# A two-layer graph kernel on one core: six tiles instead of ten between the adjacency scan and the first gather

## What is computed

```python
h = relu(layernorm(x))
# layer 0: attention by cosine of two projections, over the neighbours
raw = cosnorm(h @ Wk.T) @ cosnorm(h @ Wq.T).T
att = softmax(where(adj > 0, raw, NEG), axis=1)
prop = att @ h                       # h itself where a row has no neighbour
x = x + 0.5 * prop + 0.5 * h
# layer 1: attention by two vectors, over the same neighbours
h = relu(layernorm(x))
g = h @ W.T + b_W
e = leaky((g @ a1)[:, None] + (g @ a2)[None, :] + b_a, 0.2)
x = x + softmax(where(adj > 0, e, NEG), axis=1) @ g
```

## Time and profile before

| | |
|---|---|
| median of 3 runs | 1671.44 us (1669.94 to 1672.61) |
| the profiled execution: time | 1664.98 us |
| its span, first to last instruction | 1663.2 us |
| GpSimd (POOL) busy | 1120.6 us, 67% |
| TensorE busy (matmul) | 1140.0 us, 69% |
| VectorE busy | 1041.8 us, 63% |
| ScalarE busy | 891.0 us, 54% |
| adjacency loads on SyncE's queue | 256 of 1024 KB |
| indirect gathers issued by GpSimd | 1120 (576 + 544) |

### The profile page before, as it was taken

How to read it: one execution, slowest core, us unless ns; L and a number is a source line. 1 busy time by engine, 2 the same in 40 slices (tenths; PEclk the granted TensorE clock), 3 DMA queues, 4 the chain that set the end, 5 groups by cost and what they waited for, 6 DMA issues and landing times.

```text
span 1663.2 us, 22697 instructions
## 1 busy us (share of the span) xinstructions
PE 1140.0 (69%) x6317; PEld 898.4 (54%) x6317; DVE 1041.8 (63%) x4012; ACT 891.0 (54%) x2786; POOL 1120.6 (67%) x1170
## 2 busy tenths in 40 slices
PE   5877677777676677676556647666666767666765
PEld 3544344444444454454546537666666766666655
DVE  5976688888788887888763314444444444444444
ACT  3543455556556556556768735555555555555433
POOL 1224777777777767766777157777777777777775
PEclk9998788988989988889766657787878787878878
DMA  9999999999999999999222022222222222222222
GB/s 353 420 372 365 405 408 405 406 407 406 405 402 388 399 399 396 397 394 375 64 55 59 22 47 60 58 60 60 60 60 60 60 60 61 59 60 60 61 60 49
DMA packets 108396, 361.69 MB, mean 217 GB/s; under 512 B 24421, under 2 KB 57576, under 8 KB 75496
## 3 DMA queue, kind: packets, MB, share of 16 engines
q1 hardware_dynamic: 55272, 277.05, 41.4%
q0 software_dynamic: 35840, 74.62, 17.5%
q10 hardware_dynamic: 17152, 8.52, 1.9%
HBM read 347.38 MB, written 12.72 MB: 217 GB/s over the span
## 4 chain that ended last, share of the span: by engine, by line
POOL 35%; issue 12%; PE 2%; ACT 1%; DMA 0%; DVE 0%; POOLq 0%; ACTq 0%; DVEq 0%
POOL arena L559 18%; POOL arena L554 13%; POOL arena L968 4%; PE ps L1043 1%; PE ps L517 1%; ACT prod L1134 0%; DMA arena<-tab,idx_all 0%; PE ps L377 0%; ACT diag L1145 0%; PE ps L599 0%; DMA tab<-tw 0%; ACT arena L506 0%; ACT arena L508 0%; ACT arena L504 0%; ACT h L355 0%
## 5 line engine op out<-in xcount | busy, mean ns | idle before, releaser
L968 POOL DMA_INDIRECT arena<-tab,idx_all x576 | 564.0, 979 | 207.1 <-issue 167.7
L1012 PE MATMUL ps<-arena,fold 128*128 128x512 fp8e4 x1024 | 302.0, 427 | 194.4 <-DMA arena<-in_adj_dram 193.8
L559 POOL DMA_INDIRECT arena<-tab,idx_all x320 | 303.3, 948 | 97.5 <-issue 97.5
L554 POOL DMA_INDIRECT arena<-tab,idx_all x224 | 214.4, 957 | 111.7 <-issue 68.0
L1012 PEld LDWEIGHTS ps<-arena,fold 128*128 128x128 bf16 x1024 | 89.3, 102 | 360.2 <-DMA arena<-in_adj_dram 267.7
L1134 ACT ACTIVATE prod<-prod,arena 128x128 f32<-128x128 f32 x576 | 221.9, 388 | 34.3 <-DVE prod L1349 34.3
L686 DVE SCALAR_TENSOR_TENSOR arena<-ps,s_all,arena 128x512 f32<-128x512 f32 (+1 forms) x112 | 66.9, 633 | 252.0 <-PE ps L575 252.0
L575 PE MATMUL ps<-ident,arena 128*128 128x128 f32 x704 | 133.3, 358 | 77.6 <-DMA arena<-tab,idx_all 77.5
L517 PE MATMUL ps<-arena 128*128 128x26 f32 x704 | 103.9, 297 | 105.4 <-ACT keys L526 93.4
L629 ACT ACTIVATE arena<-arena,negm 128x517 f32<-128x517 f32 (+1 forms) x64 | 56.8, 887 | 216.4 <-DVE negm L696 216.4
L575 PEld LDWEIGHTS ps<-ident,arena 128*128 128x128 f32 x704 | 118.5, 258 | 82.7 <-DMA arena<-tab,idx_all 82.7
(11 more groups left out here) (200 smaller groups left out, 2205.2 us busy)
## 6 DMA issues: line engine op xcount, KB each, us to landing
arena<-in_adj_dram SPq DMA_DIRECT2D x256, 1024.0 KB
arena<-tab,idx_all POOLq DMA_INDIRECT x1120, 2.6
tab<-arena ACTq DMA_DIRECT2D x16, 260.0 KB, 14.5
tab<-tw ACTq DMA_DIRECT2D x32, 130.0 KB, 10.3
res<-in_x_dram SPq DMA_DIRECT2D x8, 512.0 KB, 6.6
out_dram<-arena SPq DMA_DIRECT2D x64, 64.0 KB, 1.6
prod<-in_L_gnn_Wq_dram SPq DMA_DIRECT2D x1, 64.0 KB
prod<-in_L_gnn_Wk_dram SPq DMA_DIRECT2D x1, 64.0 KB
```

The lines of the kernel that those rows point to most:

```text
L554: pool.indirect_dma_start(out=GS[h % 2][:, c, :], out_offset=None, in_=tab1, in_offset=bass.IndirectOffsetOnAxis(ap=idx_all[:, at, slot:sl ...
L559: pool.indirect_dma_start(out=GO[q][:, s, :], out_offset=None, in_=tab1, in_offset=bass.IndirectOffsetOnAxis(ap=idx_all[:, t, s:s + 1], ax ...
L968: pool.indirect_dma_start(out=G[q][:, s, :], out_offset=None, in_=tab0, in_offset=bass.IndirectOffsetOnAxis(ap=idx_all[:, t, s:s + 1], axi ...
L1012: last = nc.tensor.matmul(keys_ps[t % 2], fold[:, PIECE_BITS * f + b, :], ring8[m % RING][:, b * WORDS:(b + 1) * WORDS], start=False, stop ...
```

## The change

- `LEAD` is 3 and `AHEAD` 6: TensorE folds tile t + 7 in turn t, VectorE extracts t + 6.
- `early` has eight blocks, spread over the front (`1, 3, 4, 6, 8, 10, 12, 14`). Eight tiles are folded in the front, and only six of them extracted, decoded and compacted there; the other two wait in the two PSUM buffers. So the loop folds nothing in turns -1 and 0.
- The mask of a tile and its owner rows are made one tile later than before (`owner_mask(t + 2)`, `owners(t + 1)`); ScalarE copies the owner rows after its second-stage work; the count of the places (`offsets` on TensorE) stands before the second half of the fold.
- Own and spill slots of a gather have semaphores of their own, and GpSimd waits for the two halves of the index list apart, so the own half is gathered, multiplied and weighed without the other. `weighted` starts with the spill slots.
- Second layer: masks 0 to 3 are made on VectorE (new `masks1_vector`) in turns 64 and 65, their owner rows on TensorE in the same turns, copied at turn 66 and selected at 67. Masks 4 to 8 and their owner rows are made at the start of the second layer. `AT1` is 9, and each later selection comes one tile later on VectorE.
- The wait for the edge rows moves from the first `extract` to the end of the front.

```diff
-    AT1 = 10
+    AT1 = 9
-    LEAD = 5
+    LEAD = 3
     AHEAD = 2 * LEAD
-        edge_row = keys[0:1, :, 0:ROW]
+        edge_row = R[0][0:1, 0:2 * ROW].rearrange("p (a c) -> p a c", a=2)
...
+        def masks1_vector(dve, link, t):
+            first, n = span(t)
+            r, m = R1[t][:, 0:n * P], mask[t][:, 0:n * P]
+            nc.vector.tensor_scalar(r, iota1[:, 0:n * P], float(P * first), owner[:, t, OFF:OFF + 1], ALU.add,
+                                    ALU.is_ge).then_inc(s_R1, 1)
+            dve.wait_ge(s_R1, 3 * t + 1)
+            nc.vector.scalar_tensor_tensor(out=r, in0=iota1[:, 0:n * P], scalar=end4[:, t:t + 1], in1=r,
+                                           op0=ALU.is_lt, op1=ALU.mult).then_inc(s_R1, 1)
+            dve.wait_ge(s_R1, 3 * t + 2)
+            nc.vector.tensor_scalar(m, r, -1.0, -OUT, ALU.add, ALU.mult).then_inc(s_R1, 1)
...
+            for t in range(QT, AT1 - 1):
+                owners1_tensor(pe, t)
             edge_scores(0)
...
+            for t in range(QT, AT1):
+                masks1_scalar(act, t)
+                if t == 2 * QT - 1:
+                    copy_owners1_scalar(act, 1)
...
-        early = [1, 2, 4, 5, 6, 8, 9, 10, 12, 13]
-        assert len(early) == AHEAD and early[-1] < NB - 1
+        early = [1, 3, 4, 6, 8, 10, 12, 14]
+        assert len(early) == AHEAD + 2 and early[-1] < NB - 1
...
-                    pool.wait_ge(s_idx, 2 * t + 2)
                     if t >= GR:
                         pool.wait_ge(s_pv, t - GR + 1)
                     for s in range(SLOTS):
+                        if s in (0, K):
+                            pool.wait_ge(s_idx, 2 * t + 1 + s // K)
...
-                for t in range(-2, LAST):
-                    if t + 2 < T:
-                        owners(t + 2)
+                for t in range(-1, LAST):
+                    if t + 1 < T:
+                        owners(t + 1)
                     scan = t + AHEAD + 1
-                    if AHEAD <= scan < T:
+                    if AHEAD + 2 <= scan < T:
                         folds(scan, 0, PIECES // 2)
...
-                    if 60 <= t < 60 + AT1:
-                        owners1_tensor(pe, t - 60)
...
+                    if t in (T, T + 1):
+                        owners1_tensor(pe, 2 * (t - T))
+                        owners1_tensor(pe, 2 * (t - T) + 1)
...
-                    if 59 <= t < 59 + AT1:
-                        masks1_scalar(act, t - 59)
+                    if t == T + 2:
+                        copy_owners1_scalar(act, 0)
...
-                    if 2 <= t + 3 < T:
-                        owner_mask(t + 3)
+                    if 2 <= t + 2 < T:
+                        owner_mask(t + 2)
...
-                    if t in (65, 69):
-                        select1_vector(dve, link, (t - 65) // QT)
+                    if t in (T, T + 1):
+                        masks1_vector(dve, link, 2 * (t - T))
+                        masks1_vector(dve, link, 2 * (t - T) + 1)
+                    if t == T + 3:
+                        select1_vector(dve, link, 0)
```

More of the change, by code:

```diff
@@ L403, in adjacency_layers @@
         s_R, s_E, s_Eev, s_idx = sem("owner_mask"), sem("owner_rows"), sem("owner_rows_copied"), sem("idx_written")
-        s_g = [sem(f"l0_gathered_{q}") for q in range(GR)]
+        s_g = [[sem(f"{tag}_gathered_{q}") for q in range(GR)] for tag in ("own", "spill")]
         s_prod, s_red, s_ex = sem("l0_products"), sem("l0_scores"), sem("l0_weights")
@@ L1080, in _ @@
                         second.tensor_pr(pe, (t - 10) // 2)
-                    if AHEAD <= scan < T:
+                    if AHEAD + 2 <= scan < T:
                         folds(scan, PIECES // 2, PIECES)
-                    pair = (t + AHEAD - 3) // 2
-                    if t % 2 and LEAD <= pair < PAIRS:
-                        offsets(off_ps, pair, 1)
                 either(pe, rows_tensor, lists_tensor)
```

62 lines of the change are left out of this document (32 added, 30 removed).

## The result

The changed kernel took 1657.47 us (median of five runs, 1656.66 to 1662.78), the kernel before 1671.44 on the same chip: a ratio of 0.9929, 95% interval 0.9911 to 0.9946. On a second chip it was 0.9935 (0.9909 to 0.9961). By the ratio that is 12 us, by the medians 14 us, where 27 were forecast: inside the range of 1629 to 1664, but half the gain is missing.

A forecast was written before the change was run, and what follows sets the result against it. GpSimd's gathers were taken as the backbone, with the adjacency scan setting the pace beside it; -23 (gathers' end), -4 (drain) and 0 (second layer) made -27 us, from 1671.4 to 1644, range 1629 to 1664.

The forecast's parts named there:

- The front: Before the first gather: two tiles fewer folded there shorten it by 17 us, first gather at 138 instead of 154.9.
- Rival B: In the front: slowly landing table stores keep the first gather at 155; 1661 us in all, chance 0.17.
- The scan's end: First layer's adjacency scan: 53.5 tiles at 12.36 us from 159, last fold at 820, 23 us later than before.
- rival D: Loop beside the scan becomes too tight, VectorE lengthens each turn; at 0.6 us a turn 1678 us, chance 0.09.
- rival E: Cost moved, not removed: scan ends 46 us later instead of 23, only the drain gains; 1667 us, chance 0.06.
- The seven tiles behind the scan: Gathers after the last fold: seven tiles left instead of eleven, 11.58 us each, gathers ending at 900.
- The distance as a whole: Shorter distance from scan to gather in the first layer: gathers end at 900 instead of 923, -23 us.
- Nearer masks: Loop's masks and owner rows, only reordered: 5 us of cover in turn 33, priced at 0, bounds 0 and 1 us a turn.
- The drain: From the last products to the second layer's first gather: 37.4 us instead of 41.7, -4 us, bounds -9 and +5.
- The second layer: Masks made at its start and later selections one tile later, with 13 us of cover left: cost 0, bounds -2 and +10.

The follow-up runs named there:

- a0b: The changed kernel, unchanged, run again on another chip: 1658.82 us, 0.9935 of the kernel before.
- e1b: The changed kernel with the second layer's masks ten tiles ahead and owner rows copied and selected one tile earlier, as before: 1650.81 us, 0.9889 of the kernel before.
- f1: The changed kernel with its 16-byte tile end4 allocated behind the arena instead of ahead of it: 1645.52 us, 0.9859 of the kernel before.
- f3: The changed kernel with end4 behind the arena and the second layer's later selections as before (ten lists ahead, early): 1641.35 us, 0.9825 of the kernel before.
- h2: f3 with code0 (256 bytes per partition) moved behind the arena too: 1641.73 us, 0.9843 of the kernel before.
- h3: f1 with the second layer's masks ten lists ahead and the late selection kept: 1643.06 us, 0.9843 of the kernel before.
- h4: f1 with nine lists ahead kept and the later selections early, as in the kernel before: 1646.08 us, 0.9864 of the kernel before.
- b0b: The kernel before, unchanged, run again on the same chip as a0b: 1667.12 us.
- f4: The changed kernel with ten tiles from scan to gather as before and end4 behind the arena: 1666.95 us, 0.9987 of the kernel before.

## Why the prediction was right and wrong

**The front: right.** First gather at 141.0 for 138, fold of tile 9 at 160.8 for 159. Rival B, the slow stores, did not come: a table store lands after 12.1 us (median) where it took 14.5, and after 8.8 in `a0b`. The 7.5 us that GpSimd waits for the last store ahead of its first gather, where the earlier trace rows have 3.0, are 2.9 in `a0b`, so they are scatter. One reading was too sure: the earlier trace rows put ScalarE's 22.6 us down to "issue", not to stores, and after the change they are 18.3.

**The scan's end: the step that failed.** "53.5 tiles are to come: 159 + 53.5 x 12.36 = 820." The number of tiles and the start were right (the packets show 10.5 tiles loaded when tile 9 is folded), the 12.36 us were not: (838.3 - 160.8) / 53.5 = 12.66. I took the old turn over to the new kernel as if it were a property of the load, and it was, but of a load that begins on the right address. The prediction said that it would be wrong here "if a tile takes other than 12.4 us between folds"; it looked like rival D, in which VectorE makes the turn longer, and the scan's end, 41 us later than before, looked like rival E's 46. It was neither: with `end4` behind the arena the turn from tile 20 to tile 63 is back at 12.33 to 12.41 us in six kernels, all with the new order of the loop.

The shift is not all of the miss. By the prediction's own count, from the fold of tile 9 on, the three traces with the shift (the changed kernel's two and `e1b`) have 12.63 to 12.66 us, and the five without it `f1` 12.49, `f3` 12.44, `h2` 12.47, `h3` 12.49 and `h4` 12.52. So the shift is some 0.17 of the 0.30 us, 9 us over the scan; 0.08 to 0.16 remain, 4 to 9 us, of which 0.05 is scatter (`b0b` has 12.41 where the first trace had 12.36). The remainder lies before tile 20. What makes it stays open.

In `f1`, which is what my sum described, the last fold ends at 825.4 for 820 and the last gather at 904.2 for 900. The gathers' end is 17 us late in the changed kernel and 4 in `f1`, whose first gather is also 5 us earlier. That the time of `f1` is 1645.5 for 1644 is luck: its profiled span is 1646.7 where the sum had 1636, and the sum of spans was carried to the medians by an offset of 6.5 us that `f1` doesn't have (its profiled execution lies above its median).

**The seven tiles behind the scan: right.** Gather 57 starts at 836.37 beside the last fold; 916.8 - 836.4 = 80.4 us, forecast 7 x 11.58 = 81.

**The distance as a whole: right.** The sum had -23. Undoing it alone costs 18.9 us with the shift in both kernels, and 1.28%, 21 us, with it in neither (`f4` against `f1`).

**Nearer masks: right, by the wrong measure of safety.** They cost next to nothing (in `f4` the last fold ends at 799.8, in the two traces of the kernel before at 796.9 and 798.4), but the cover that I read off one turn isn't what makes it so. TensorE's wait for masks, by line 1031 before and line 1049 after:

```profile
  DVE R L1326: 78.3, 20
```

```profile
  DVE R L1343: 148.2, 33
```

It nearly doubled, and the scan didn't notice, because TensorE has to wait for data anyway: ahead of its folds it stood 461.5 us for the adjacency before and 383.3 after. Beside this a small slip: VectorE's slack is (535 - 447) / 43 = 2.0 us a turn, not 1.5.

**The drain: better than forecast, -9 for -4.** I had the last tile's weights 10.7 us behind the last products, its weighted sum at 24 and the next layer at 37.4. The timelines of VectorE, ScalarE and TensorE show the products, the start of the weights and the last part of tile 63's weighted sum:

```profile
919.02 0.56 DVE L1367 TENSOR_TENSOR prod<-arena 128x384 f32<-128x384 f32 x1 [3.31 <-DMA arena<-tab,idx_all]
```

```profile
929.95 0.39 ACT L1154 ACTIVATE prod<-prod,arena 128x128 f32<-128x128 f32 x1
```

```profile
937.31 1.50 PE L1061 MATMUL ps<-arena,diag 128*128 128x130 f32 x12
```

The weights start 10.9 us behind the products, as forecast; the weighted sum is done at 938.8, 19.8 us behind them, not 24; the layer starts at 32.4. The term that was mis-sized is TensorE's work between the weights and that sum: I had it end 7.6 us behind the weights, and it ended 3.2 behind. Weighted sum 61 and owner rows 2 and 3 (928.2 to 934.1) ran during ScalarE's weights (929.9 to 935.7).

**The second layer: wrong in the step, inside its bounds.** I priced it at 0, bounds -2 and +10, by asking who would wait. GpSimd waited no longer than before. The 7.6 us came as longer gathers, a kind of cost the sum had no line for, although carry its sign: a median of 945 ns and a maximum of 1712.

The pieces of the profiled executions add up. Forecast -27; the gathers' end +17, of which some 12 are the shift by the difference to `f1`; the second layer +8; the drain -5: -7, and the spans differ by -7.7. The range of 1629 to 1664 held the result by luck: it was drawn from the bounds of the front and the drain, and neither the scan's rate nor the second layer's longer gathers was a reason for it. The best kernel is `f3`, the change with `end4` declared last and with ten lists ahead: 0.9825, 1641.35 us, some 17 us faster than the change as it was made. `h2` and `h3` (0.9843 both) can't be told from it.

## What to carry over

Before you take a rate over from the old profile to the new kernel, compare the addresses, not only the instructions: in this kernel a 16-byte tile declared ahead of the buffers that the loads write cost 0.6 to 0.8%, and declared behind them nothing. Read a saturated queue by engine time per MB, which is independent of how many packets fit into the span; it showed in one row that the loads had become dearer, where the waits pointed to TensorE and VectorE. And on the engine that sets the time look at the mean duration of its instructions too, since a neighbour can lengthen them without any wait appearing.

## What was unexpected of the hardware

- Moving the buffers of the adjacency loads by 32 or 64 bytes makes their 8 KB packets about 1.5% dearer (322 to 327 ns on average; the median from 309 to 314 or 315), and with saturated DMA engines the whole kernel 0.5 to 0.8% slower. A move of 256 bytes cost nothing that could be measured (`h2`).
- An indirect gather on GpSimd that starts inside a wide two-input VectorE operation ends 0.81 to 0.92 us after that operation does, in up to 1.7 us instead of 0.945; one that is already under way isn't lengthened. A difference in phase, kept up over a layer, made 7 us.
- The same programs took 18 to 27% longer on one chip, at DMA shares of 0.78 to 0.95 and 295 to 359 GB/s beside the scan instead of 1.02 and 400, while the front ran there as elsewhere (0.99 and 390 GB/s for the kernel before). The order of the changes was another there: the late selection with nine lists ahead, which costs 4 to 8 us elsewhere, cost 77 us.
